# A decoder layer on one core: cross scores of a sequence in one call, new PSUM banks, and a new written-out order of attention and feed-forward calls

## The reference

```
x = layernorm(x + self_attention(x))          # 16 heads, q, k and v of 64, causal
x = layernorm(x + cross_attention(x, ctx))    # 16 heads of 8, padding mask, biases
x = layernorm(x + moe(x))                     # 8 experts, F = 256, top 2 of a sparsemixer router
moe: logits = x @ router_w.T ; out = sum_e dense_w[:, e] * ((silu(x @ gate_e.T) * (x @ up_e.T)) @ down_e.T)
```

## Time and profile before

| | us |
|---|---|
| median of 3 runs | 261.14 (260.43 to 262.89) |
| the profiled execution | 260.83 |
| its span, first to last instruction | 258.9 |
| TensorE busy (matmul) | 242.2 (94%) |
| VectorE busy | 191.3 (74%) |
| ScalarE busy | 167.9 (65%) |
| GpSimd busy | 92.7 (36%) |

### The profile page before, as it was taken

One profiled execution on the slowest core, in us unless ns is written; L12 is line 12 of the kernel. 1 busy time (PEld: TensorE's weight loads), 2 busy tenths in 40 slices (PEclk: granted clock), 3 DMA queues, 4 the chain that ended last, 5 costly groups with the idle time before them and its releaser, 6 DMA issues.

```text
span 258.9 us, 6792 instructions
## 1 busy us (share of the span) xinstructions
PE 242.2 (94%) x2242; PEld 209.6 (81%) x2242; DVE 191.3 (74%) x933; ACT 167.9 (65%) x558; POOL 92.7 (36%) x151
## 2 busy tenths in 40 slices
PE   6988999999999999999989998966989999999992
PEld 6977887887887887887857867845889999999992
DVE  2875778689589589689699696774467876675885
ACT  3678498988988988988979886438544833333000
POOL 3257947337338339439453360130011000010111
PEclk9999999999999999999999999997799999999998
DMA  6998000000000000000000000000000000000000
GB/s 202 365 366 327 6 0 4 0 4 1 3 1 3 0 4 1 3 0 4 4 0 3 1 0 4 0 4 0 3 0 0 3 1 4 0 23 0 22 23 20
DMA packets 6722, 9.09 MB, mean 35 GB/s; under 512 B 1056, under 2 KB 5280, under 8 KB 6304
## 3 DMA queue, kind: packets, MB, share of 16 engines
q1 hardware_dynamic: 4176, 7.09, 7.5%
q10 hardware_dynamic: 2512, 1.57, 2.2%
HBM read 8.14 MB, written 0.52 MB: 33 GB/s over the span
## 4 chain that ended last, share of the span: by engine, by line
PE 82%; DVE 8%; issue 3%; POOL 3%; ACT 2%; POOLq 0%; ACTq 0%; DVEq 0%
PE bank L1209 10%; PE bank L897 10%; PE bank L898 8%; PE bank L899 8%; PE bank L1045 6%; PE bank L988 6%; PE bank L1117 6%; PE bank L1061 6%; PE bank L1014 5%; PE bank L1030 4%; PE bank L1076 4%; PE bank L1135 2%; DVE probsT_s L628 1%; PE bank L928 1%; PE bank L927 1%
## 5 line engine op out<-in xcount | busy, mean ns | idle before, releaser
L313 POOL TENSOR_TENSOR probs_s<-probs_s,rec_sum_s 128x512 f32<-128x512 f32 x32 | 33.3, 1041 | 54.8 <-DVE rec_sum_s L622 54.7
L442 ACT ACTIVATE probs_s<-masked_s,nmax_s 128x128 f32<-128x128 f32 x128 | 49.8, 393 | 3.9 <-DVE nmax_s L614 3.5
L445 ACT ACTIVATE probs_c<-masked_c,nmax_c 128x128 f32<-128x128 f32 x128 | 40.3, 392 | 5.3 <-DVE nmax_c L614 5.3
L483 ACT ACTIVATE silu<-bank 128x256 f32<-128x256 f32 x54 | 20.5, 384 | 30.5 <-PE bank L899 30.5
L897 PE MATMUL bank<-ctx_hi,gu_hi 128*128 128x256 f32 x128 | 39.6, 310 | 0.0
L898 PE MATMUL bank<-ctx_lo,gu_hi 128*128 128x256 f32 x128 | 36.6, 286 | 0.0
L899 PE MATMUL bank<-ctx_hi,gu_lo 128*128 128x256 f32 x128 | 36.5, 285 | 0.0
L614 DVE CUSTOM_DVE_ANT_0 masked_s<-bank,causal 128x128 f32<-128x128 f32 x128 | 29.5, 286 | 4.1 <-PE bank L988 4.0
L614 DVE CUSTOM_DVE_ANT_0 masked_c<-bank,mask_add 128x128 f32<-128x128 f32 x128 | 28.9, 285 | 0.1
L897 PEld LDWEIGHTS bank<-ctx_hi,gu_hi 128*128 128x128 f32 x128 | 25.1, 196 | 1.5 <-issue 1.4
L898 PEld LDWEIGHTS bank<-ctx_lo,gu_hi 128*128 128x128 f32 x128 | 25.0, 196 | 0.0
(11 more groups left out here) (158 smaller groups left out, 595.7 us busy)
## 6 DMA issues: line engine op xcount, KB each, us to landing
raw<-in_gateT SPq DMA_DIRECT2D x1, 1024.0 KB, 9.4
raw<-in_upT SPq DMA_DIRECT2D x1, 1024.0 KB, 11.6
down_sb<-in_down SPq DMA_DIRECT2D x1, 1024.0 KB, 13.7
raw<-in_wvT SPq DMA_DIRECT2D x1, 512.0 KB, 5.9
ctxT_all<-in_ctxT SPq DMA_DIRECT2D x1, 512.0 KB, 7.2
masked_c<-in_mask ACTq DMA_DIRECT2D x1, 512.0 KB, 8.5
wo_sb<-in_woT SPq DMA_DIRECT2D x1, 512.0 KB, 8.2
x_tok<-in_x ACTq DMA_DIRECT2D x1, 512.0 KB, 17.6
```

Source lines behind the costliest of these rows:

```text
L313: pool.tensor_tensor(probs_s[:, g % 2], probs_s[:, g % 2], spread(rec_sum_s[:, 4 * g:4 * g + 4], 2, S), ALU.mult).then_inc(normed, 1)
L442: last = act.activation(probs_s[:, g % 2, i, :], masked_s[:, g % 2, i, :], ACT.Exp, scale=-1.0, bias=nmax_s[:, h:h + 1], accum_out=rsum_s[ ...
L445: last = act.activation(probs_c[:, g % 2, i, :], masked_c[:, g % 2, i, :], ACT.Exp, scale=-1.0, bias=nmax_c[:, h:h + 1])
```

## The change

1. `score_c(m)` is one call for each sequence: four matmuls, one a strip of 32 rows, each to a bank of its own. It was two calls of two.
2. Every use of a PSUM bank names its bank anew; no bank has a role. The order of calls is written out call by call for TensorE, ScalarE, VectorE and GpSimd, in place of the loop. Where a bank's last reader isn't known to be done by the order alone, an explicit wait stands before the call (`pe.wait_ge`). Semaphores that counted all groups are split into one for each group, so that groups may run in any order (for instance `turn("c", 3, 2)` before `turn("c", 2, 2)`).
3. Evacuations change engine. The values (`evac_v`), the three of the four `evac_qk` of a step that ScalarE had, `evac_qc` and `evac_ccatT` go from ScalarE to VectorE. The turned groups 0 and 2 of self-attention, the second half of `evac_cat` and `evac_oc` go from VectorE to ScalarE, as does the one `evac_qk` that VectorE had.
4. All 32 gate/up products of chunks 0 and 1 stand in the written-out order: one before the last `score_c`, 31 behind it (11 of these in a row or nearly so at the end). Before it was seven ahead of the last `score_c`, 15 among the calls behind it, ten at the end. The instructions of the routing weights are ten blocks (`rank_0` to `rank_9`) among `hidden` calls.
5. The results `Y` of the main loop use X0, X1 and OC (they used T0, T1 and OS), its gates T1, Y0, Y1 and T0.

The main loop itself, all arithmetic and all loads are as before. At the start GpSimd makes the key bias (`key_bias`) ahead of `normalise(0, 0)`; it stood behind it.

```
-            def score_c(m, a):
-                if not on(m):
-                    return
...
-                for r in range(2):
-                    rows = slice(32 * (2 * a + r), 32 * (2 * a + r + 1))
-                    pe.matmul(PAIR[a][r][:], qc[rows, :], k_own[rows, m % 2].rearrange("p s t -> p (s t)"),
-                              start=True, stop=True).then_inc(scored["c"], 1)
+            def score_c(m, *banks):
+                pe.wait_ge(cq_evac, m + 1)
+                pe.wait_ge(k_own_done, m + 1)
+                for j in range(NG):
+                    rows = slice(32 * j, 32 * (j + 1))
+                    pe.matmul(banks[j][:], qc[rows, :], k_own[rows, m % 2].rearrange("p s t -> p (s t)"),
+                              start=True, stop=True).then_inc(scored["c"][j], 1)
...
+            def turn(kind, g, n, b):
+                pe.wait_ge(normed[g] if kind == "s" else exped["c"][g], n + 1)
+                for i in range(4):
+                    last = pe.transpose(b[:, i * S:(i + 1) * S], (probs_s if kind == "s" else probs_c)[:, g % 2, i, :], ident[:])
+                last.then_inc(turned[kind][g], 1)
...
             for i in range(WARM):
                 pe.transpose(OC[:, 0:P], ident[:], ident[:])
-            for n in range(B + 2):
-                turn_s(0, n)
...
+            score_c(0, X1, Y1, T1, X0)
+            next_qk(1, 2, OS)
+            pe.wait_ge(qk_evac[3], 2)
+            score_s(2, 0, Y0, OC)
+            pe.wait_ge(maxed["c"][1], 1)
+            mix_s(1, 0, Y1)
+            pe.wait_ge(maxed["c"][0], 1)
+            turn("s", 2, 1, X1)
+            turn("s", 3, 1, T0)
+            pe.wait_ge(maxed["s"][1], 3)
+            next_qk(2, 2, OC)
+            pe.wait_ge(turned_evac["s"][2], 2)
+            turn("c", 0, 0, X1)
+            mix_s(1, 1, T0)
+            turn("c", 1, 0, Y0)
+            pe.wait_ge(maxed["c"][3], 1)
+            next_qk(2, 3, X0)
+            project_out_s(1, T0)
+            pe.wait_ge(qk_evac[3], 3)
+            score_s(2, 1, X0, OS)
+            turn("s", 0, 2, Y1)
+            pe.wait_ge(turned_evac["c"][1], 1)
+            turn("s", 1, 2, Y0)
+            project_v(2, 0, X1)
+            turn_x1(1, T1)
+            project_v(2, 1, OS)
+            pe.wait_ge(turned_evac["s"][0], 3)
+            turn("c", 2, 0, Y1)
+            next_qk(2, 0, OC)
+            pe.wait_ge(v_evac[0], 3)
+            turn("c", 3, 0, X1)
+            project_qc(1, X0)
+            pe.wait_ge(v_evac[1], 3)
+            mix_c(0, 0, OS)
+            mix_c(1, 0, OS)
+            score_c(1, T1, T0, Y0, X0)
...
+            score_c(7, X1, OC, Y0, X0)
+            pe.wait_ge(oc_evac, 7)
+            gate_up(1)
+            pe.wait_ge(res2_done, 6)
+            turn_oc(6, T1)
+            gate_up(2)
+            pe.wait_ge(maxed["c"][0], 8)
+            gate_up(3)
...
+            route(7, Y1)
+            gate_up(20)
+            pe.wait_ge(hid_done, 19)
+            gate_up(21)
+            pe.wait_ge(logit_evac, 8)
+            gate_up(22)
```

The other engines' programs are written out in the same way, for ScalarE for instance:

```
+            exp("c", 0, 4)
+            evac_cat(5, 0, OC)
+            exp("c", 1, 4)
+            evac_qk(5, 1, T1)
+            evac_turned("s", 2, 5, X1)
+            evac_oc(3, OS)
+            evac_turned("c", 0, 4, Y1)
+            exp("s", 1, 6)
```

More of the change, by code:

```diff
@@ L67, in build_decoder @@
     NSLOT = B - 2
[L68 to L81, removed]
+    NFILL = 32
     NTANH = 10
-    for table in (GATE_PE, GATE_ACT, GATE_DVE):
-        assert sum(table.values(), []) == list(range(NFILL))
     with ExitStack() as ctx:
@@ new lines, in _ @@
+            turn("s", 3, 0, X1)
+            pe.wait_ge(cat_done[0], 1)
+            score_s(1, 0, Y1, X0)
+            mix_s(0, 1, X1)
+            next_qk(0, 3, T1)
+            pe.wait_ge(maxed["s"][0], 2)
+            project_out_s(0, Y1)
+            pe.wait_ge(qk_evac[3], 1)
+            score_s(1, 1, T1, OS)
+            next_qk(1, 1, Y0)
+            pe.wait_ge(qk_evac[0], 1)
+            project_v(1, 1, T0)
+            next_qk(1, 0, X0)
+            turn_x1(0, T1)
+            turn("s", 0, 1, Y1)
@@ new lines, in _ @@
+            project_v(6, 1, X0)
+            turn_x2(1, X1)
+            turn_x1(5, OC)
+            turn("s", 0, 6, T0)
+            pe.wait_ge(turned_evac["c"][2], 5)
+            project_qc(5, T1)
+            project_out_c(3, OC)
+            mix_c(1, 4, OS)
+            score_c(5, Y1, T1, Y0, X0)
+            pe.wait_ge(turned_evac["s"][0], 7)
+            turn("c", 3, 4, T0)
+            pe.wait_ge(res2_done, 4)
+            turn("s", 3, 6, OC)
+            mix_s(6, 0, X1)
+            mix_c(2, 4, OS)
@@ new lines, in _ @@
+            mix_c(3, 4, OS)
+            turn("s", 2, 6, T0)
+            pe.wait_ge(turned_evac["s"][3], 7)
+            score_s(7, 0, OC, Y1)
+            mix_s(6, 1, T0)
+            turn_oc(4, X1)
+            turn("c", 1, 5, T1)
+            pe.wait_ge(maxed["s"][1], 8)
+            turn_x2(2, Y1)
+            project_out_s(6, Y0)
+            route(1, T0)
+            pe.wait_ge(maxed["c"][3], 6)
+            turn("c", 0, 5, X0)
+            pe.wait_ge(logit_evac, 2)
+            score_s(7, 1, T0, X1)
@@ new lines, in _ @@
+            project_qc(6, Y1)
+            project_out_c(4, X1)
+            mix_c(2, 5, OS)
+            mix_c(3, 5, OS)
+            pe.wait_ge(v_evac[0], 8)
+            score_c(6, Y1, OC, X0, T1)
+            turn("s", 2, 7, T0)
+            pe.wait_ge(res2_done, 5)
+            route(2, X1)
+            mix_s(7, 0, Y0)
+            pe.wait_ge(maxed["c"][1], 7)
+            turn("s", 3, 7, OC)
+            turn_oc(5, OS)
+            pe.wait_ge(maxed["c"][0], 7)
+            turn("c", 1, 6, Y1)
```

1750 lines of the change are left out of this document (1168 added, 582 removed).

## The result

The changed kernel takes 242.13 us (median of 4 runs, 241.78 to 242.31) beside 261.03 for the kernel before; the ratio is 0.926, with an interval of 0.922 to 0.931. The profiled execution took 241.99 us, its span is 240.2.

What follows compares the result with a forecast made beforehand. TensorE was taken to bound the kernel, with waits before the main loop. From the profiled 260.83 us: work -7.5, old losses -17.8, new losses +10.5, in total -14.8, gives 246.0; the median forecast is 246.3, range 239 to 256.

Steps and rivals of the forecast that it cites:

- The cross scores: Eight calls of four strips at 1.13 us, 9.04 us in place of 15.97, save 6.9 us of TensorE's work.
- The start: Up to the first score_c: 28.4 us of TensorE work, of 3.6 us of old loss 1.5 stay; arrival at 36.6.
- 1 us more: Before the first score_c: extra cost if the work ahead of the first turn doesn't cover GpSimd's normalisation.
- The seven stretches: From first to last score_c: 112.5 us of TensorE work plus 5 us of new waits, 1.5 each in fifth and sixth.
- ScalarE's 87%: Check between score_c calls: if ScalarE could again be used for only 87%, 118 us instead of 112.5, a loss of 5.9.
- The tail: From the last score_c to the main loop: some 28.5 us of TensorE work and 4 us of waiting; clock stays up.
- The 17.8 us of old losses: TensorE's time lost before the old kernel's main loop, 195.4 us for 177.6 of work; all expected to go.
- The clock's part: Old tail, 178.0 to 185.5 us: granted clock of 0.54 behind TensorE's idle time, counted as 3.4 us lost.
- swaps ten evacuations for ten: ScalarE between score_c calls: evacuations given up and taken on balance, apart from evac_qc and evac_ccatT, which it gives up.
- everything lands in time: Rival, whole kernel: new losses of 5 us in place of 10.5, so 240.8 us (237 to 241.5); chance 0.12.
- The strips don't overlap: Rival at score_c: 2.12 us a call, no saving, 254.3 us; its chance is within 0.18 shared with waits changing place.
- The banks become the bound: Rival at the 64 turns: late evacuations hold TensorE up 0.44 us each, 28 us, so 264 and more; slower 0.05.

## Why the prediction was right

The direction and the mechanism were right, and the size was 3.9 us short (span 240.2 for 244.1). By the stations that it named:

- *The cross scores, -6.9 us.* Right. Eight groups of eight records, 1.07 to 1.14 from start to start; undone in the new order, the split costs 8.2 us of span, 8.6 from the first cross scores on.
- *The start, "of these 3.6 us of loss I leave 1.5".* Too little: `score_c(0)` came at 38.08 instead of 36.6. I had seen that `key_bias` moves ahead of `normalise(0, 0)` and put its end near 18 us; it was at 20.0, because I priced the call and not the load that it waits for. That is "1 us more" of the missing cover, and 0.4 besides; the reordered loads took 1.37 back. (Up to a microsecond of this term differs from execution to execution, with the load.)
- *The seven stretches, 112.5 of work and "I put 5 us".* They took 114.7. TensorE was idle for 0.48 of that; if the rest is work, it was under-counted by 1.7 and the loss over-estimated by 4.5, and if the records hide waits, by less, down to the net 2.8. The step that was mis-sized is this 5, with its check by ScalarE's 87%: a busy share that an engine happened to have in the old order is no ceiling. ScalarE's load was counted well (103 for 106.1), it went to 93%, and taking 8.4 us from it gained nothing. VectorE was counted too high: about 16 us of 17 in a full stretch, where it was 13.9 to 16.4.
- *The tail, 28.5 of work and "I leave 4 us of waiting".* It took 30.4 for 32.5, with 1.02 us idle. The six products more and VectorE's room were right, and the clock stayed at 1.00.
- *The main loop, nothing.* 57.0 for 56.8: the routing weights were in time.
- *The 17.8 us of old losses.* By stations I expected 36.6 + 117.5 + 32.5 = 186.6 and 56.8 behind it, 243.4; the sum over losses gave 244.1. So 0.7 is the difference of my own two counts. The clock's part, 3.4, was 2.0 when tried by itself.

Over-estimated losses of 2.8 (stretches, net) and 2.1 (tail), less 1.5 (start) and 0.3 (main loop), and the 0.7 of the two counts make the 3.9 (rounded).

What I foretold of the waits was wrong: the largest is not between the fifth and the seventh `score_c` with ScalarE as releaser, but at 20.10 with GpSimd and, behind it, a load. There are 0.45 us of idle time where I looked for the most.

And one step was right only by luck. I costed the exchange of evacuations at nothing but load ("swaps ten evacuations for ten"). The new order with the old engines, in queues not tuned for them, is 13.8 us slower at nearly the same load. The gain of 18.7 doesn't split into parts that add up: the strips in the old order cost 5.8, the strips in the new order are worth 8.2, and order and strips without the exchange are worth 4.9. The new placing of the gate/up products was not undone by itself.

Of the rivals, "everything lands in time" (240.8, with 237 to 241.5) came closest: the measured 242.13 is 0.6 above its range and 1.3 from its value, nearer than my own forecast, and I had given it a chance of 0.12. "The strips don't overlap" fell by the rows of eight records. "The banks become the bound" didn't come about in the changed kernel, but waits for a bank are real: in the old order the four-strip call waited for one (1.63 us for 1.13) and the kernel became slower. The Trainium skill, "TensorEngine Tiling (Array Packing)", section "PSUM Bottleneck", says that the evacuation may become the bottleneck once four strips run at once. The changed kernel's trace doesn't show that, with TensorE idle for 0.48 of 114.7 us, and the trace of the old order shows it only in part: ScalarE had been idle for 0.45 us right before the evacuation in question, so the bank was late by the order of the calls and not for want of an engine.

## What to carry to other kernels

Test the room of an engine by adding work to it, at the places that matter, and not by its busy share: here 7 to 9 us more work cost 0.33 us for each on ScalarE, which was busy for 93%, and 0.7 to 0.8 on VectorE, which was busy for 85%. Faster operations on the engine that bounds paid here only with banks and evacuations placed for them: the strips cost 5.8 us in the old order and gave 8.2 in the new one, so a part tried alone can look worthless. When a call is moved ahead of another on a queue, look up what its semaphore counts: a wait for eight loads of which three are read cost 1.4 us. And hold two executions against each other by stretches, as an equal span can hide a difference behind an earlier start.

## What the runs showed of the hardware

- Semaphore waits on TensorE's queue that the order already meets cost little, but not nothing: 116 more of them made a stretch of 114.68 us 0.87 us longer.
- The granted clock fell to 0.54 behind a stretch of 8.2 us in which TensorE was idle for 3.35, and stayed at 1.00 when the idle time there was filled with transposes of no use (idle for 0.67). Such work in place of a wait made the old kernel 2.0 us shorter in the span, 2.7 in the median.
- The stretch from the first to the last cross scores took 114.68 to 114.71 us in four kernels that differ in their start, in the tail or in ScalarE's load (97.77 for 106.14 us). So none of these bounds it; of VectorE this says nothing.
- The same load can land over a microsecond earlier or later in another execution: `key_bias`, which waits for it, began between 15.38 and 16.78 us.
